# A graph layer's gathered blocks, summed by DMAs that add instead of by matmuls

## What is computed

```python
xn = layernorm(x)                        # no gain, no bias
deg = segment_sum(1, dst)                # the layer adds one more loop per node
norm = rsqrt(deg)[src] * rsqrt(deg)[dst]
out = segment_sum((xn @ W)[src] * norm[:, None], dst) + b
x1 = x + where(out > 0, out, prelu_a * out)
z = layernorm(x1)
# router over the mean of z, the two best of 8 experts for all tokens
y = sum_of_two(w_e * (gelu(z @ W1[e] + b1[e]) @ W2[e] + b2[e]))
return x1 + layer_norm(y + z, gamma, beta)
```

## Time and profile before

| | |
|---|---|
| time, median of 3 runs | 1091.21 us (1087.17 to 1091.28) |
| span of the profiled execution | 1087.7 us |
| busy in it: PE, DVE, ACT, POOL | 1029.0, 799.5, 686.9, 548.6 us |
| stretch of the blocks' sums (first to last matmul of line 1860) | about 82 to 783 us |
| instructions | 21027 |

### The profile page before, as it was taken

How to read it: one execution, slowest core, us unless ns; L and a number is a source line. 1 busy time by engine, 2 the same in 40 slices (tenths; PEclk the granted TensorE clock), 3 DMA queues, 4 the chain that set the end, 5 groups by cost and what they waited for, 6 DMA issues and landing times.

```text
span 1087.7 us, 21027 instructions
## 1 busy us (share of the span) xinstructions
PE 1029.0 (95%) x6895; PEld 863.2 (79%) x6896; DVE 799.5 (74%) x1631; ACT 686.9 (63%) x1515; POOL 548.6 (50%) x516
## 2 busy tenths in 40 slices
PE   8899999999899998988989989899989999999997
PEld 6777788778687776866778868687789999999996
DVE  6898778667577776685767657577578878878886
ACT  6794676667476766665666757576495655646551
POOL 4103576777778777777777777764101111111111
PEclk9999999999899999999999989999999999999999
DMA  9087455656656666666666656665421111111101
GB/s 288 26 298 246 134 169 153 194 168 184 184 168 185 190 190 183 194 181 180 181 174 184 180 167 187 179 193 157 165 65 49 40 53 48 43 43 43 48 30 34
DMA packets 72551, 157.08 MB, mean 144 GB/s; under 512 B 11557, under 2 KB 38063, under 8 KB 72463
## 3 DMA queue, kind: packets, MB, share of 16 engines
q0 software_dynamic: 34896, 114.72, 36.8%
q1 hardware_dynamic: 37566, 41.22, 11.6%
HBM read 130.23 MB, written 25.67 MB: 143 GB/s over the span
## 4 chain that ended last, share of the span: by engine, by line
PE 83%; ACT 6%; DVE 4%; another core or an unknown queue 3%; issue 3%; DMA 1%; ACTq 0%; DVEq 0%; SPq 0%
PE banks L1860 36%; PE banks L1976 11%; PE banks L1836 10%; PE banks L1878 9%; PE banks L1990 8%; PE banks L1995 4%; PE banks L1712 2%; ACT adj L1570 2%; ACT hot_row L1587 1%; PE banks L1807 1%; DVE hot_src L918 1%; ACT hot_row L1594 1%; ACT gf L1642 1%; ACT gh L1640 1%
## 5 line engine op out<-in xcount | busy, mean ns | idle before, releaser
L746 POOL DMA_INDIRECT row<-h_table,lists x385 | 464.0, 1205 | 207.4 <-issue 101.7
L1860 PE MATMUL banks<-tab,adj 128*128 128x512 f32 x1862 | 461.4, 397 | 2.7 <-ACT adj L1575 1.3
L1860 PEld LDWEIGHTS banks<-tab,adj 128*128 128x128 f32 x1862 | 354.1, 191 | 83.1 <-issue 2.3
L1570 ACT CAST adj<-banks 128x784 fp32r<-128x784 f32 x296 | 232.4, 814 | 228.3 <-PE banks L1836 162.1
L918 DVE TENSOR_TENSOR hot_src<-iota_src,turned 128x2048 bf16<-128x2048 bf16 x152 | 185.8, 1222 | 158.6 <-PE banks L1836 117.0
L1836 PEld LDWEIGHTS banks<-hot_key,hot_src 128*128 128x128 bf16 x2368 | 115.4, 98 | 64.3 <-issue 52.4
L1836 PE MATMUL banks<-hot_key,hot_src 128*128 128x98 bf16 x2368 | 139.9, 210 | 22.9 <-ACT adj L1570 12.9
L918 DVE TENSOR_TENSOR hot_key<-iota_key,turned 128x1568 bf16<-128x1568 bf16 x152 | 147.4, 969 | 0.0
L1990 PE MATMUL banks<-W2s,gh 128*128 128x512 f32 x384 | 136.0, 395 | 0.6 <-DVE pre L1388 0.6
L1878 PE MATMUL banks<-row,hot_row 128*128 128x512 f32 x385 | 125.3, 433 | 10.9 <-ACT hot_row L1594 7.4
L1640 ACT ACTIVATE gh<-banks,b1e 128x384 fp32r<-128x384 f32 (+1 forms) x136 | 79.7, 586 | 87.2 <-PE banks L1976 87.0
(11 more groups left out here) (227 smaller groups left out, 1165.7 us busy)
## 6 DMA issues: line engine op xcount, KB each, us to landing
h_table<-tab SPq DMA_DIRECT2D x5, 2048.0 KB, 9.1
xin<-in_x SPq DMA_DIRECT2D x49, 128.0 KB
x_dram<-x SPq DMA_DIRECT2D x49, 128.0 KB
row<-h_table,lists POOLq DMA_INDIRECT x385
x1f<-x_dram POOLq DMA_DIRECT2D x16, 384.0 KB, 3.7
out<-res SPq DMA_DIRECT2D x48, 128.0 KB, 1.7
W1a<-in_W POOLq DMA_DIRECT2D x8, 512.0 KB, 6.4
xs<-in_x SPq DMA_DIRECT2D x2, 1536.0 KB, 13.5
```

What stands on the lines that cost most here:

```text
L746: g.indirect_dma_start(out=row[:, u, :].bitcast(F32), out_offset=None, in_=h_table, in_offset=bass.IndirectOffsetOnAxis(ap=lists[:, m % 2, ...
L1570: s.copy(adj[k][:, :].rearrange("p (q n) -> p q n", n=P)[:, :, at:at + 2 * BANK_NODES].rearrange("p q (b n) -> p q b n", b=2), bank_pairs[ ...
L1860: last = mm(acc[k][:, :], adj[k][:, q * P:(q + 1) * P], tab[:, q, :], start=(at == 0), stop=(at == T - 1), skip_group_check=True)
```

## The change

The blocks are dealt anew: every fifth is gathered instead of every fourth, so 9 gathered (5, 10, ... 45) and 40 dense. And a gathered block is no longer summed by TensorE.

- Partition p belongs to node p of the block. In round k (`add_round`, 40 rounds, `SUMMED`) one indirect DMA on GpSimd's queue takes for every node the source row of its k-th edge, 1 KB from the new table `h_rows`, and **adds** it (`compute_op=ALU.add`) to one of five partial sums on chip (`partial`, `PARTIALS`). A node with fewer edges is given a row past the last node, which is zero. Round k waits until round k-5 has landed, since both add to the same partial sum.
- Partial 0 starts as the node's own row (`load_own`, on SP), the other four are cleared by ScalarE (`clear_partials`).
- Edges beyond the 40th of a node, up to 128 in a block, are placed by a few small matmuls and sums in the prologue (`extra`, `extra_end`, `before_extra`), gathered by one DMA (`load_extra_rows`) and added by one matmul of 128x256 (`sum_extra`). Their lists are nine small indirect DMAs before the rounds.
- VectorE makes the row numbers (`node_rows`, three short instructions), one one-hot (`one_hot_extra`) and adds the partials (`add_partials`, three additions, then `x1_sum` on the last two).
- `h_rows` holds the full float32 row: SP stores the high halves (six DMAs) and GpSimd's queue then adds the low halves in memory (`add_low_rows`, six DMAs with `accum_op=ALU.add`), each after the high ones of its pair of parts have landed. All rounds wait for all of these.
- Gone are `gather`, `add_gathered`, `hot_rows`, `own_nodes`, the lists, the ring of slots, and `h_table` from this path. `load_W1(0, EARLY_W1)` and the late constants wait for an epilogue instead of the last gathered matmul.

```diff
-GCH = 35
-GFIRST, GCYCLE = (5,), 4
-RING = 10
+SUMMED = 40
+GFIRST, GCYCLE = 5, 5
+PARTIALS = 5
...
+    def rounds(i):
+        m, j = divmod(i, SLOTS_PER)
+        return [(m, k) for k in range(SUMMED * j // SLOTS_PER, SUMMED * (j + 1) // SLOTS_PER)] if m < NGATH else []
...
-                    sp.dma_start(h_table[lo * P:hi * P, :].rearrange("(t p) d -> p t d", p=P), tab[:, lo:hi, :].bitcast(F32)).then_inc(h_kept, 16)
+                    sp.dma_start(h_rows[lo * P:hi * P, :].rearrange("(t p) d -> p t d", p=P), tab[:, lo:hi, 0:D].bitcast(F32)).then_inc(hi_stored[i // 2], 16)
...
+                def load_extra_rows(m):
+                    k = m % 2
+                    if m >= 2:
+                        pool.wait_ge(extra_summed, m - 1)
+                    g.indirect_dma_start(
+                        out=extra_row[:, k, :], out_offset=None, in_=h_rows,
+                        in_offset=bass.IndirectOffsetOnAxis(ap=extra_src[:, m:m + 1], axis=0),
+                        bounds_check=last_row).then_inc(extra_row_in[k], 16)
+                def add_low_rows(i):
+                    lo, hi = TABLE_PARTS[i]
+                    if lo < HELD:
+                        pool.wait_ge(lo_fixed, hi)
+                    else:
+                        pool.wait_ge(lo_made, hi - HELD)
+                    pool.wait_ge(hi_stored[i // 2], 32)
+                    g.dma_start(h_rows[lo * P:hi * P, :].rearrange("(t p) d -> p t d", p=P), tab[:, lo:hi, D:2 * D].bitcast(F32),
+                                accum_op=ALU.add).then_inc(h_summed, 16)
+                def add_round(m, k):
+                    u, a = m % 2, k % PARTIALS
+                    if k == 0:
+                        pool.wait_ge(node_row_made, m + 1)
+                        pool.wait_ge(own_in[u], m // 2 * 16 + 16)
+                        pool.wait_ge(partial_clear, m + 1)
+                    if m or k >= PARTIALS:
+                        pool.wait_ge(partial_in[a], landings(m, k) - 16)
+                    g.indirect_dma_start(
+                        out=partial[:, u, a, :], out_offset=None, in_=h_rows,
+                        in_offset=bass.IndirectOffsetOnAxis(ap=node_row[:, u, k:k + 1], axis=0),
+                        bounds_check=last_row, compute_op=ALU.add).then_inc(partial_in[a], 16)
...
+                for i in range(len(TABLE_PARTS)):
+                    add_low_rows(i)
+                pool.wait_ge(h_summed, 16 * len(TABLE_PARTS))
+                pool.wait_ge(extra_src_in, 16 * NGATH)
                 for i in range(ND):
-                    ends(i)
-                pool.wait_ge(row_used, NGATH * GCH)
+                    if i % 2 and i + 5 < ND:
+                        load_edges((i + 5) // 2)
+                    if i % SLOTS_PER == 1 and i // SLOTS_PER + 2 < NGATH:
+                        load_node_src(i // SLOTS_PER + 2)
+                    for m, k in rounds(i):
+                        add_round(m, k)
+                        if k == SUMMED - 1:
+                            load_extra_rows(m)
+                pool.wait_ge(epi, GATHERED[-1] * EPI + (2 * EPI + 2))
                 load_W1(0, EARLY_W1)
...
+                def add_partials(m):
+                    k = m % 2
+                    for a in range(PARTIALS):
+                        dve.wait_ge(partial_in[a], block_landings(m, a))
+                    v.tensor_tensor(partial[:, k, 0:2, :], partial[:, k, 0:2, :], partial[:, k, 2:4, :], ALU.add).then_inc(partials_added, 1)
+                    dve.wait_ge(extra_summed, m + 1)
+                    v.tensor_tensor(partial[:, k, 4, :], partial[:, k, 4, :], extra_ps, ALU.add).then_inc(partials_added, 1)
+                    dve.wait_ge(partials_added, m * 3 + 2)
+                    v.tensor_tensor(partial[:, k, 1, :], partial[:, k, 1, :], partial[:, k, 4, :], ALU.add).then_inc(partials_added, 1)
...
+                def sum_extra(m):
+                    pe.wait_ge(hot_extra_made, m + 1)
+                    pe.wait_ge(extra_row_in[m % 2], m // 2 * 16 + 16)
+                    if m:
+                        pe.wait_ge(partials_added, m * 3 - 1)
+                    mm(extra_ps, hot_extra[:, m % 2, :], extra_row[:, m % 2, :], start=True, stop=True, skip_group_check=True).then_inc(extra_summed, 1)
...
-                        add_gathered(i, s)
                         add_rows(i, cuts[s], cuts[s + 1])
+                        if s == 2 and DENSE[i] - 1 in GATHERED:
+                            sum_extra(GATHERED.index(DENSE[i] - 1))
```

More of the change, by code:

```diff
@@ L131, in gnn_ffn_kernel, with landings, block_landings @@
     LAST = (ND - 1) % 2
[L132 to L150, removed]
+    assert DENSE[ND - 3:] == [T - 3, T - 2, T - 1] and ROWS <= HALF
+    assert len(LISTED) == 1 and BOTH == P and SUMMED < P and T * P > N and ND % 2 == 0
+    def rounds(i):
+        m, j = divmod(i, SLOTS_PER)
+        return [(m, k) for k in range(SUMMED * j // SLOTS_PER, SUMMED * (j + 1) // SLOTS_PER)] if m < NGATH else []
+    def landings(m, k):
+        return (m * len(range(k % PARTIALS, SUMMED, PARTIALS)) + k // PARTIALS + 1) * 16
+    def block_landings(m, a):
+        return landings(m, range(a, SUMMED, PARTIALS)[-1])
     assert T % 4 == 1 and T == NG * GT + 1 and NG % 2 == 0
@@ L969, in _ @@
             dve.wait_ge(deg_kept, 1)
+            for slots, blocks in LISTED:
+                v.tensor_scalar(extra[:, slots], deg_loop[:, blocks], float(-SUMMED - 1), 0.0, ALU.add, ALU.max).then_inc(extra_made, 1)
+                v.tensor_scalar(one_few[:, 1, slots], deg_loop[:, blocks], -1.0, float(SUMMED), ALU.add, ALU.min).then_inc(extra_made, 1)
             dve.wait_ge(square_made, FIRST)
@@ L1155, in rows_of @@
                     beside = b > 2 and d - 1 in GATHERED
+                    m = GATHERED.index(d - 1) if beside else 0
                     hot_step(b, 0)
@@ L1185, in _ @@
                 last_tiles(between)
-                v.tensor_copy(ident_r[:, :], ident[:, :]).then_inc(consts, 1)
+                for m in range(2):
+                    node_rows(m)
+                dve.wait_ge(extra_edge_made, 2)
+                for m in range(2):
+                    one_hot_extra(m)
                 for b in range(1, ND):
@@ L1613, in _ @@
                 keep_first(BANKS - 1)
+                for m in range(2):
+                    clear_partials(m)
                 for b in range(1, ND):
@@ L1773, in _ @@
             mm(flag_ps[0:1, 0:1], unsorted[:, :], ones[:, 0:1], start=True, stop=False)
-            mm(flag_ps[0:1, 0:1], over_wide[:, :], ones[0:1, 0:1], start=False, stop=False)
+            mm(flag_ps[0:1, 0:1], over_wide[:, :], ones[:, 0:1], start=False, stop=False)
             mm(flag_ps[0:1, 0:1], lost[0:ROWS, :], ones[0:ROWS, 0:1], start=False, stop=True).then_inc(flag_made, 1)
+            pe.wait_ge(before_extra_made, 1)
+            for slots, blocks in LISTED:
+                mm(cum_ps[:, EXTRA_AT + NGATH:EXTRA_AT + 2 * NGATH], total[:, :], before[:, 0, blocks], start=True, stop=True, skip_group_check=True)
+            for m in range(NGATH):
+                for i in range(2):
+                    at_m = EXTRA_AT + i * NGATH + m
+                    last = mm(cum_ps[:, at_m:at_m + 1], before_extra[:, m, :], one_few[:, i, m:m + 1], start=False, stop=True, skip_group_check=True)
+            last.then_inc(extra_placed, 1)
             tiles(at + 4, SPLIT)
```

272 lines of the change are left out of this document (146 added, 126 removed).

## The result

The changed kernel takes **1244.44 us** (median of 4 runs, 1241.52 to 1245.84) against 1090.63 us of the kernel before (4 runs, 1087.17 to 1091.28): a ratio of **1.144**, 95% interval 1.1395 to 1.1479. The forecast was 1064 us, its range ended at 1165, and it had put 0.38 on slower. The kernel is slower by more than the range allowed.

A forecast was written before the change was run, and what follows sets the result against it. TensorE bounded the old kernel; GpSimd's queue would pace the new: start 118 + rounds 551 + other DMAs 51 + tail 35 = 755 us against 782.6, 27 less, giving 1064 us, range 1018 to 1165.

The forecast's parts named there:

- GpSimd, the new pace: Step pricing GpSimd's queue: 360 adding rounds at 1.53 us each, the gather's price, with nothing extra for adding.
- GpSimd sets the pace: In the block-summing stretch GpSimd's queue needs 67 us a cycle, more than the 58 to 61 of the engines.
- The mean, not the floor, is the price, since VectorE works beside it: A round's issue was priced at the gather's mean of 1.205 us, not its floor of 1.006.
- The other indirect DMAs at 1.6 us, 33 of them: Loads of edges, node lists and extra rows in GpSimd's queue; 32 counted at 1.6, 51 us.
- The start at 118 us: First round, after the low halves are added in memory, was put at 118 us, bounds 97 and 124.
- The tail of 35 us: End of the stretch after the last round: 6 us for landing and extra rows, 29 us of TensorE's remaining work.
- The engines alone between 700 and 740: TensorE and VectorE, if not held by GpSimd, would end the block-summing stretch between 700 and 740 us.
- The 64 us of waits and slow issue: Part of TensorE's 701 us stretch beyond its 637 us of matmuls, kept whole in the new estimate of 637.
- the engines' case: Rival: rounds stay near 1.35 us, TensorE and VectorE pace; 1009 to 1049 us, middle 1030, chance 0.15.
- The landings pace: Rival: adding rounds land after 9.1 us, so 1.83 us a round; 1172 us, up to 1226, chance 0.15.
- The issue is dearer: Rival: every round costs GpSimd 0.10 to 0.20 us more; 1100 to 1136 us, chance 0.25.
- The early load of W1 costs nothing: W1's load moves about a window later, still before the stretch ends; counted as nothing, at most 14 us.

The follow-up runs named there:

- experiment 2: The changed kernel with each adding round covering only 64 of the 128 rows: 1210.71 us.
- experiment 3: The changed kernel with rounds adding rows of 512 bytes instead of 1 KB: 1248.90 us.
- experiment 10: The changed kernel with rounds that copy instead of add, and only 64 of the 128 rows: 1059.26 us.
- Experiment 9: The changed kernel with rounds that copy instead of add: 1057.84 us, 1.007 of the kernel before on the same chip.
- experiment 6: The changed kernel without the six DMAs that add the low halves in memory, rounds waiting for the first stores alone: 1221.16 us.
- experiment 11: The changed kernel with 38 rounds a gathered block instead of 40, the rest going to the extra list: 1209.05 us.
- experiment 5: The changed kernel with only 20 of the 40 rounds issued for each gathered block: 998.37 us.

## Why the prediction was wrong

**The step that failed** is in "GpSimd, the new pace": "I take nothing for it, the gather being nearest in kind", for what adding costs in issue. It measured 0.53 us at the floor, which lies even above the upper bound of 0.45, the whole excess of an indirect over a direct DMA. The argument took descriptors to be what GpSimd's time goes into and the bound from their number; experiments 2, 3 and 10 show that the larger part is there with half the rows and with half the bytes. On average the round cost 2.02 and not 1.53 us, 360 x 0.49 = 176 us. With it, and with the start as measured, the sum reads 121 + 727 + 51 + 35 = 934 us against 936.2. Experiment 9 is the direct check: with the adding taken away the same order ends at 748.1 where the sum said 755. Its 1058 us lie near the forecast's 1064, but on a chip where the kernel before takes 1052 and not 1091, so there the copies gain nothing; that they would have gained the forecast's 27 us on the first chip needs GpSimd's pace to be the same on both, which no run shows directly.

Point by point:

- *GpSimd sets the pace*: right. Experiments 6 and 11 move the end by about what they take from its queue; experiment 5 takes 364 us from it and moves the end by 246, until TensorE paces.
- *The mean, not the floor, is the price, since VectorE works beside it*: right in kind and size. The mean lies 0.18 us above the floor, near the gather's 0.20, and the rounds beside VectorE's one-hots carry it (below).
- *The other indirect DMAs at 1.6 us, 33 of them*: right. With 40 x 2.02 they make 86.7 of the 87.2 us of a period.
- *The start at 118 us*: 121.3, and experiment 6 shows that 27.7 us of it belong to the low halves. Their landings (median 16.6 us, the last 22.4 in the chain) are longer than the 13.9 us of the stores, so the doubt about them was in place; the bound of 124 held.
- *The tail of 35 us*: 37, of which 3.9 for the landing in place of 4.6.
- *The engines alone between 700 and 740*: too late; 690 in experiment 5. The 64 us of waits and slow issue were carried over whole, and half of them are gone: 603 us of stretch hold 40 x 14.33 = 573 and 30 of the rest. It cost the forecast nothing, since GpSimd hides it; it made the engines' case (1009 to 1049) too slow against the 998 measured.
- *The landings pace*: the mechanism didn't occur. It needed landings over 7.6 us; those seen took 3.7 to 6.7, and no round of the changed kernel waited for one. By the Trainium skill, Collectives: The Full Stack, section "The bandwidth ceiling: the fold count and why AG ≠ RS ≠ AR", a ReduceScatter is slower than an AllGather because the add needs two source reads. The DMA engines' work here fits that: the same 68.90 MB of GpSimd's queue took them 35.0% of 1242.8 us with adding and 23.9% of 1055.0 without, 435 against 252 us. But it was never what the kernel waited for.
- *The issue is dearer*: the right rival with too small a size. It was priced at 0.10 to 0.20 us (1100 to 1136) and the 0.45 of the upper bound was only lent to the landings' case; 0.45 alone gives 1064 + 162 = 1226, close to the result, and the range should have reached there.
- *The early load of W1 costs nothing*: near enough; the part behind the stretch grew by 1.5 us.

## What to carry to other kernels

When work moves from an engine that paces to GpSimd's DMA queue, the count of DMAs times their issue can be the new pace. Here halving the bytes saved nothing, and halving the rows saved 34 us where halving the rounds saved 246. And an operation the trace doesn't show (here an indirect DMA that adds) needs its full upper bound in the range, not the price of its nearest kin. The break-even was 0.08 us a round: when so small an error in an unmeasured price decides the sign, the number of rounds is what to tune. The other DMAs of the queue wait with them, as the loads of edges did with seven blocks. Five gathered blocks in place of nine leave GpSimd under TensorE's pace and turn a loss of 14% into a gain of 4%.

## What the runs showed of the hardware

**Adding costs GpSimd half as much again.** An indirect DMA of 128 rows takes it 1.007 us at the least to issue when it copies (experiment 9) and 1.534 when it adds; of 64 rows 0.952 and 1.402 (experiments 10 and 2); an adding one costs with rows of 512 bytes what it costs with 1 KB (experiment 3). Direct DMAs that add had about the same floor: line 795, six transfers from SBUF into memory, 1.532 at the least and 2.421 at the most. The direct copies took 0.557 and 0.764, but they are smaller, and no run has the same transfer as a copy.

**GpSimd's issue grows beside some work of VectorE.** Timeline of the changed kernel, both engines:

```profile
833.98 1.56 POOL L807 DMA_INDIRECT partial<-h_rows,node_row  x1 [0.31 <-issue]
834.15 0.48 DVE L1129 SCALAR_TENSOR_TENSOR agg<-banks,dinv,neg 128x256 f32<-128x256 f32 x1
...
838.68 1.21 DVE L982 TENSOR_TENSOR hot_src<-iota_src,turned 128x2048 bf16<-128x2048 bf16 x1
839.10 2.20 POOL L807 DMA_INDIRECT partial<-h_rows,node_row  x1 [0.31 <-issue]
839.81 0.96 DVE L982 TENSOR_TENSOR hot_key<-iota_key,turned 128x1568 bf16<-128x1568 bf16 x1
...
841.28 1.22 DVE L982 TENSOR_TENSOR hot_src<-iota_src,turned 128x2048 bf16<-128x2048 bf16 x1
841.60 2.33 POOL L807 DMA_INDIRECT partial<-h_rows,node_row  x1 [0.30 <-issue]
842.42 0.97 DVE L982 TENSOR_TENSOR hot_key<-iota_key,turned 128x1568 bf16<-128x1568 bf16 x1
```

Beside these one-hots, which read two tensors of SBUF, a round takes 2.20 to 2.33 us; at 833.98, beside the short operations of an epilogue, and after 895 us, with VectorE idle, it takes 1.56. Not every round beside a one-hot is slow, but over all 360 rounds of this trace the split is clear. The 146 that no one-hot of line 982 overlaps take 1.56 us on average and 1.67 at most. The 117 with over 1.1 us of one-hots beside them take 1.86 on average, from 1.55 to 2.61. The kernel before has the same split in its gathers, 1.04 against 1.57 us. In windows of all GpSimd's work:

```profile
821.00:877.00 56.00, 56.00 (x429) 45.19 (x428) 50.91 (x89) 24.66 (x42) 48.08 (x27) 0.98 0.50 80
877.00:903.00 26.00, 2.71 (x12) 1.88 (x10) 0.00 (x0) 1.12 (x2) 21.07 (x14) 0.65 0.56 83
```

48.08 / 27 = 1.78 us an instruction while VectorE is busy for 51 of 56 us, 21.07 / 14 = 1.50 while it does nothing. The Trainium skill, GPSIMD Engine Reference, section "1. Specifications", says that GpSimd shares its SBUF interfaces with VectorE and meets contention from instructions with two SBUF inputs; the rounds agree. TensorE's work alone is not it: 35 of the 146 rounds without a one-hot have TensorE busy for over 80% of their time and take 1.58 us on average. But no run takes the one-hots away and leaves the rest. With it goes that GpSimd is a little faster while VectorE waits: 1.812 us a round in experiment 5, where VectorE hardly rests, 1.716 in the changed kernel.

**The clock fell in the waits and didn't matter.** In the window above in which TensorE stood still the granted clock was 0.65 of full speed on average, so at its lower level, 1.2 GHz in place of 2.4, for most of that time. Over the stretch it was 0.86, against 0.98 before and 1.00 in experiment 5. The matmuls that it slowed lay in the same periods as the waits for GpSimd, which took up the loss.
